# The ternary of the down weights in the first four neighbour steps of a fused GNN and FFN block, with later bias adds, earlier low parts and another ring of PSUM banks

## Chip, cores and metric

One Trainium2 chip, one of its cores. The metric is the device time of one execution in microseconds (us), the median of several runs. Lower is better. The engines are named as in the profile: PE is TensorE, DVE is VectorE, ACT is ScalarE, POOL is GpSimd and SP is SyncE, which here issues the DMAs.

## What is computed

```python
def _L0_gnn_ref(x, src, dst, W_self, W_neigh, b):          # x: 1250 x 512, 20000 edges
    msg_sum = jax.ops.segment_sum(x[src], dst, num_segments=N_NODES)
    deg = jax.ops.segment_sum(jnp.ones((src.shape[0],), x.dtype), dst, num_segments=N_NODES)
    neigh = msg_sum / jnp.maximum(deg, 1.0)[:, None]
    h = x @ W_self + neigh @ W_neigh + b
    h = jnp.where(h >= 0, h, LEAKY_SLOPE * h)
    norm = jnp.sqrt(jnp.sum(h * h, axis=1, keepdims=True))
    return h / jnp.maximum(norm, EPS)

def _quantize_weight(w, group_size):                       # groups of 128
    o, i = w.shape
    wg = w.reshape(o, i // group_size, group_size)
    scale = jnp.mean(jnp.abs(wg), axis=-1, keepdims=True) + EPS
    wq = jnp.clip(jnp.round(wg / scale), -1.0, 1.0) * scale
    return wq.reshape(o, i)

def _L0_ffn_ref(x, w_gate, w_up, w_down):                  # gate, up: 1408 x 512; down: 512 x 1408
    gate = _bitlinear(x, w_gate)
    up = _bitlinear(x, w_up)
    h = jax.nn.silu(gate) * up
    return _bitlinear(h, w_down)

x = x + _L0_gnn_ref(_layernorm(x, axis=-1), src, dst, L0_gnn_W_self, L0_gnn_W_neigh, L0_gnn_b)
x = x + _L0_ffn_ref(_layernorm(x, axis=-1)[None], L0_ffn_w_gate, L0_ffn_w_up, L0_ffn_w_down)[0]
```

## The kernel before

The 1250 nodes are ten tiles of 125 (NT = 10, TP = 125). The work has three stages. Each engine has its own program, written out by hand in the order of the code; semaphores tie them together, and every engine works strictly through its own list.

**Stage 1 (to about 121 us).** PE multiplies the normalized x by the two GNN weights (L1208) and builds a 1250 x 1250 matrix of edge counts, `a_t`, from one-hot matrices (L1167). `y` = x W_neigh is kept as a high and a low part (`y_hi`, `y_lo`), `z` = x W_self in SBUF. Beside it, the weights of the FFN are made ternary. They come in 34 loads of up to four blocks of 128 x 128 (jobs). For each job ACT takes the magnitudes and their sum (`abs_of`, L690), POOL makes from the sums of a load its thresholds (`scales_of`, L612), and DVE makes the ternary block (`ternary_of`, L901). Magnitudes have two slots (`MAGS`): those of a load wait for the ternaries of the load two before. Raw weights have four slots. Gate and up weights and the first 3 of 12 down loads are done in stage 1 (`LOADS1` = 25 loads); nine down loads (4, 3, 4, 4, 4, 3, 4, 4 and 3 jobs) are left. Their magnitudes go to `mag_late`, which may be written once the inverse degrees of the first six tiles are made (L1029, L1031).

**Stage 2, the neighbour steps (about 122 to 178 us).** For each node tile n, PE forms the neighbour sum of 20 matmuls (L1250) in bank 4 or 5. Then DVE, in step n: `neighbour_sum(n)` (L1040) adds the sum, divided by the degree, to `z`, for which POOL must have added the bias (L620); `residual(n - 1)` with `leak(n)` in its middle (L1046, L1058, bn_stats L1061, bn_aggr L1063); `shift1(n - 2)` (L1068, L1070); and the low part of a tile, `x1_low` (L1075). ACT, in step n: the square of tile n and its root (L785, L787), the root of the variance of tile n - 1 (L749), the high part of tile n - 3 (`x1_high`, L762), the normalizing of tile n - 2 (`normalize1`, L755). PE transposes normalized tile n - 3 after neighbour sum n (L1156).

The late ternaries are spread by `down_jobs(n)`: one load, then two, then one, and so on. ACT takes the magnitudes of `down_jobs(n)` at the end of step n, DVE the ternaries of `down_jobs(n - 1)` at the end of its step n. POOL adds all ten biases first and then makes the nine sets of thresholds:

```python
            for t in range(NT):
                pool.wait_ge(z_out, t + 1)
                nc.gpsimd.tensor_tensor(z[:, t, :], z[:, t, :], bias_b[0:TP, :], ALU.add).then_inc(z_done, 1)
            for l in range(LOADS1, len(loads)):
                scales_of(l)
```

**Stage 3, the FFN (from about 178 us).** The work is cut into 33 units (128 FFN columns by 3 or 4 node tiles) of 12 pieces (G0 to G3, U0 to U3, D0 to D3). Each piece is two matmuls (high and low part of the input, L1320) into one PSUM bank; ACT or DVE then takes it, scaled, into an accumulator (`take`, L808, L1114). Piece i uses bank `RING[i % 7]` and waits until piece i - 7 is taken. The first seven wait for what used the bank before, in a table in the code: banks 1 and 0 for the low parts of tiles 5 and 6 (`xlo_done` 6 and 7), banks 4 and 5 for neighbour sums 8 and 9 to be read (`hsum` 9 and 10), bank 3 for the last square, banks 2 and 6 for nothing that is late. Bank 7 carries the transposes of tiles 7 to 9 and of the ternary weights.

Of the kernel before, what the change touches and what calls it, by code (L numbers as in the profile page):

```python
# [31 lines left out]
ALU = mybir.AluOpType  # L32
# [11 lines left out]
def gnn_ffn(nc, x, src, dst, w_self, w_neigh, bias, w_gate, w_up, w_down, out):  # L44
# [3 lines left out]
    TP = 125  # L48
    NT = N // TP
# [55 lines left out]
    z = place("z", [TP, NT, D], F32, "xz")  # L105
# [62 lines left out]
    bias_b = small("bias_b", [P, D], F32)  # L168
# [21 lines left out]
    with ExitStack() as ctx:  # L190
# [72 lines left out]
        loads = []  # L263
# [70 lines left out]

        def down_jobs(n):

            lo, hi = (LOADS1 + max(0, min(NL, 3 * i // 2)) for i in (n, n + 1))
            return range(load_end[lo - 1], load_end[hi - 1])

# [39 lines left out]
        index = {p: i for i, p in enumerate(pieces)}  # L381
        RING = [2, 6, 1, 0, 4, 3, 5]
        added = {}
# [186 lines left out]
        def _(pool):  # L570
# [37 lines left out]
            def scales_of(l):  # L608

                js = slice(load_end[l] - loads[l][1], load_end[l])  # L610
                pool.wait_ge(abs_done, load_end[l])
                nc.gpsimd.tensor_scalar(thr[:, js], absum[:, js], 0.5 / P, 0.5 * Q_EPS, ALU.mult, ALU.add).then_inc(scales, 1)  # L612
# [4 lines left out]
            pool.wait_ge(joined, NB - 1)  # L617
            for t in range(NT):
                pool.wait_ge(z_out, t + 1)
                nc.gpsimd.tensor_tensor(z[:, t, :], z[:, t, :], bias_b[0:TP, :], ALU.add).then_inc(z_done, 1)  # L620
            for l in range(LOADS1, len(loads)):
                scales_of(l)

# [40 lines left out]
        def _(act):  # L664
# [111 lines left out]


            for n in range(NT):
                if n == NT - 1:
# [18 lines left out]
                if n == 0:  # L798
                    degree_out(2)
                for j in down_jobs(n):  # L800
                    abs_of(j)

# [66 lines left out]
        def _(dve):  # L869
# [203 lines left out]
            def x1_low(t):  # L1073
# [3 lines left out]
                                        ALU.subtract).then_inc(xlo_done, 1)  # L1077

            for n in range(NT):
                neighbour_sum(n)  # L1080
                if n >= 1:
                    residual(n - 1, between=n)
                else:
                    leak(n)
                if n >= 2:
                    shift1(n - 2)
                if n >= 4:
                    x1_low(n - 4)
                for j in down_jobs(n - 1):
                    ternary_of(j)  # L1090
                if n == 2:
                    inverse_degrees(DEG[2][0], DEG[2][1], 3, 2)
            shift1(NT - 2)
            x1_low(6)

# [250 lines left out]
```

## Time and profile before

| | |
|---|---|
| median of 3 runs | 363.95 us (363.95 to 364.2) |
| the profiled execution | 365.24 us |
| its span | 363.3 us |
| PE busy | 329.8 us (91%) |
| DVE busy | 304.6 us (84%) |
| ACT busy | 238.0 us (66%) |
| POOL busy | 163.1 us (45%) |

The chain that ended last is 58% PE, 26% DVE and 10% ACT; its largest lines are the FFN matmuls L1320 (39%) and L1208 (7%) and L1250 (5%). The profiled execution is 1.3 us longer than the median of the runs. A share of busy time is an average over three stages with different limits; the change lies in stage 2 and at the start of stage 3.

### The profile page before, as it was taken

Reading aid. Unit: us, or ns where it says so; the run is one execution under the profiler, and the core shown is the slowest. Engines: PE = TensorE matmul, PEld = TensorE weight load, DVE = VectorE, ACT = ScalarE, POOL = GpSimd, SP = SyncE. Lnnn points to the kernel's source line nnn. Section 1 sums busy time; section 2 is a strip of 40 time slices with the busy share of each in tenths; the row PEclk is TensorE's granted clock in tenths of the full one; section 3 lists DMA queues with packets and bytes.
Section 4 is the critical chain, followed back from the end, with each engine's and each line's share of the span. In section 5 each row is a group of like instructions: output and inputs, shape, how many; then the busy total and the mean of one; then the engine's idle time right before and its main releaser. Section 6 shows DMA issues by size and latency. Waiting matters only on the chain.

```text
span 363.3 us, 5834 instructions
## 1 busy us (share of the span) xinstructions
PE 329.8 (91%) x1623; PEld 249.6 (69%) x1623; DVE 304.6 (84%) x789; ACT 238.0 (66%) x637; POOL 163.1 (45%) x223
## 2 busy tenths in 40 slices
PE   1997879899999999999687999999999999999992
PEld 0443335554545578777476898989899898889991
DVE  3569999899889248999696998999999989999994
ACT  2155958899787136774656768668777678676670
POOL 7000000110010590110003466888788787799992
PEclk9999999999999999999988999999999999999998
DMA  7961322233232001200000000000000000000215
GB/s 226 291 159 33 86 58 78 68 88 87 59 82 79 3 3 35 74 22 2 0 1 2 0 3 0 3 0 0 2 3 2 0 0 3 0 3 0 73 44 169
DMA packets 9412, 16.69 MB, mean 46 GB/s; under 512 B 1062, under 2 KB 1886, under 8 KB 9378
## 3 DMA queue, kind: packets, MB, share of 16 engines
q1 hardware_dynamic: 9300, 16.21, 15.9%
q8 instruction: 14, 0.23, 0.3%
q14 instruction: 20, 0.16, 0.2%
q10 hardware_dynamic: 78, 0.08, 0.1%
HBM read 13.73 MB, written 2.56 MB: 45 GB/s over the span
## 4 chain that ended last, share of the span: by engine, by line
PE 58%; DVE 26%; ACT 10%; issue 3%; POOL 1%; DVEq 0%; ACTq 0%; POOLq 0%
PE bank L1320 39%; PE bank L1208 7%; PE bank L1250 5%; DVE tq_gu L901 4%; DVE hot_dst L1005 3%; ACT mag_early L690 3%; DVE tq_d L901 2%; DVE hot_src L996 2%; ACT a_t L742 2%; DVE bn L1061 2%; ACT hot_src L675 2%; DVE x_sb L1058 2%; DVE z L1040 1%; PE bank L1232 1%; PE bank L1156 1%
## 5 line engine op out<-in xcount | busy, mean ns | idle before, releaser
L1320 PE MATMUL bank<-x_hi,t_gu 128*128 128x378 f32 (+1 forms) x264 | 96.9, 367 | 3.6 <-DVE x_lo L1075 2.8
L1320 PE MATMUL bank<-x_lo,t_gu 128*128 128x378 f32 (+1 forms) x264 | 95.5, 362 | 0.0
L1208 PE MATMUL bank<-w_sb,xnT 128*125 128x512 f32 x160 | 86.9, 632 | 4.8 <-ACT z L725 4.1
L1114 DVE SCALAR_TENSOR_TENSOR g_acc<-bank,nscale,g_acc 128x378 f32<-128x378 f32 (+1 forms) x99 | 64.3, 650 | 12.1 <-PE bank L1320 10.8
L612 POOL TENSOR_SCALAR thr<-absum 128x4 f32<-128x4 f32 (+1 forms) x34 | 10.7, 315 | 121.5 <-ACT mag_early L690 97.2
L1114 DVE SCALAR_TENSOR_TENSOR u_acc<-bank,nscale,u_acc 128x378 f32<-128x378 f32 (+1 forms) x99 | 64.1, 647 | 0.0
L633 POOL TENSOR_TENSOR acc<-acc,d_one 128x378 f32<-128x378 f32 (+1 forms) x58 | 60.9, 1052 | 0.1
L643 POOL TENSOR_TENSOR hh<-sg,u_acc 128x378 f32<-128x378 f32 (+1 forms) x32 | 35.1, 1098 | 57.4 <-ACT sg L830 57.3
L1320 PEld LDWEIGHTS bank<-x_hi,t_gu 128*128 128x128 f32 x264 | 51.1, 193 | 8.1 <-DVE x_lo L1075 3.5
L1320 PEld LDWEIGHTS bank<-x_lo,t_gu 128*128 128x128 f32 x264 | 51.0, 193 | 3.6
L1167 PEld LDWEIGHTS bank<-hot_dst,hot_src 128*125 128x125 bf16 x157 | 20.8, 137 | 42.0 <-DVE hot_dst L1005 23.0
L1320 PE MATMUL bank<-h_hi,t_d 128*128 128x378 f32 (+1 forms) x132 | 48.2, 365 | 0.1
L1320 PE MATMUL bank<-h_lo,t_d 128*128 128x378 f32 (+1 forms) x132 | 46.6, 353 | 0.0
L1250 PE MATMUL bank<-y_hi,a_t 125*125 125x512 f32 x100 | 40.1, 401 | 0.8 <-DVE a_t L970 0.8
L690 ACT ACTIVATE mag_early<-raw 128x128 f32<-128x128 f32 x99 | 29.5, 301 | 16.8 <-DVE tq_gu L901 15.2
L1114 DVE SCALAR_TENSOR_TENSOR acc<-bank,nscale,acc 128x378 f32<-128x378 f32 (+1 forms) x62 | 39.5, 646 | 0.0
L1250 PE MATMUL bank<-y_lo,a_t 125*125 125x512 f32 x100 | 39.4, 394 | 0.0
L652 POOL TENSOR_TENSOR h_lo<-hh,h_hi 128x378 fp32r<-128x378 f32 (+1 forms) x32 | 35.1, 1096 | 3.4 <-ACT h_hi L847 1.9
L808 ACT ACTIVATE d_one<-bank,nscale 128x378 f32<-128x378 f32 (+1 forms) x58 | 35.2, 611 | 2.0 <-PE bank L1320 1.9
L808 ACT ACTIVATE g_acc<-bank,nscale 128x378 f32<-128x378 f32 (+1 forms) x33 | 20.2, 613 | 24.0 <-PE bank L1320 24.0
L1005 DVE TENSOR_SCALAR hot_dst<-iota_w,key 128x140 bf16<-128x140 uint16 (+4 forms) x150 | 34.2, 268 | 1.0 <-PE bank L1167 1.0
L1208 PEld LDWEIGHTS bank<-w_sb,xnT 128*125 128x125 f32 x160 | 25.4, 196 | 10.0 <-ACT z L725 5.1
(136 smaller groups left out, 558.5 us busy)
## 6 DMA issues: line engine op xcount, KB each, us to landing
raw<-in_L_ffn_w_gate SPq DMA_DIRECT2D x11, 256.0 KB, 2.7
raw<-in_L_ffn_w_up SPq DMA_DIRECT2D x11, 256.0 KB, 2.6
out_x<-x_sb SPq DMA_DIRECT2D x10, 224.0 KB
raw<-in_L_ffn_w_down SPq DMA_DIRECT2D x8, 256.0 KB, 2.7
x_sb<-in_x SPq DMA_DIRECT2D x1, 1344.0 KB
w_sb<-in_L_gnn_W_neigh SPq DMA_DIRECT2D x1, 1024.0 KB, 6.0
w_sb<-in_L_gnn_W_self SPq DMA_DIRECT2D x1, 1024.0 KB, 7.3
raw<-in_L_ffn_w_down SPq DMA_DIRECT2D x4, 192.0 KB, 2.3
```

The source lines that it names most:

```text
L633: nc.gpsimd.tensor_tensor(to, to, d_one[:, o, slot, 0:width(u)], ALU.add).then_inc(d_added, 1)
L643: nc.gpsimd.tensor_tensor(hh[:, u % 2, 0:w], sg[:, u % 2, 0:w], u_acc[:, u % 2, 0:w], ALU.mult).then_inc(h_done, 1)
L652: nc.gpsimd.tensor_tensor(h_lo[:, u % h_slots, 0:w], hh[:, u % 2, 0:w], h_hi[:, u % h_slots, 0:w].bitcast(F32), ALU.subtract).then_inc(hlo ...
L690: nc.scalar.activation(mag_of(j), raw_of(j), ACT.Abs, accum_out=absum[:, j:j + 1]).then_inc(abs_done, 1)
L808: nc.scalar.activation(to, bank_of(u, what)[:, 0:width(u)], ACT.Copy, scale=nscale[:, j:j + 1]).then_inc(act_took, 1)
L901: nc.vector.scalar_tensor_tensor(out=tq_of(j), in0=mag_of(j), scalar=thr[:, j:j + 1], in1=raw_of(j), op0=ALU.is_gt, op1=ALU.mult).then_inc ...
L1005: nc.vector.tensor_scalar(to, numbers, key[:, c:c + 1], None, ALU.is_equal).then_inc(hot_made, 1)
L1114: nc.vector.scalar_tensor_tensor(out=to, in0=bank_of(u, what)[:, 0:w], scalar=nscale[:, j:j + 1], in1=to, op0=ALU.mult, op1=ALU.add).then_ ...
L1167: nc.tensor.matmul(bank[k % 3][0:TP, 0:NT * WIN].rearrange("p (s d) -> p s d", d=WIN)[:, :, lo:hi], hot_src[:, c // SB % SBS, c % SB, 0:TP ...
L1208: last = nc.tensor.matmul(to[0:TP, :], xnT[:, t, k * TP:(k + 1) * TP], w_sb[:, k, half * D:(half + 1) * D], start=k == 0, stop=k == KD - 1)
L1250: last = nc.tensor.matmul(bank[4 + n % 2][0:TP, :], a_t[:, s, n * TP:(n + 1) * TP], y[:, s, :], start=s == 0 and y is y_hi, stop=s == NT - ...
L1320: last = nc.tensor.matmul(to, w, parts[h], start=h == 0, stop=h == 1)
```

## The change

The nine late loads are handed out by a list, `PHASE` = [3, 3, 2, 1]. Group 0 (three loads) stands on ACT and on DVE ahead of the neighbour steps; group n + 1 stands at the end of step n on both. POOL's bias adds stand one tile ahead of the steps, between the thresholds of the groups. The low part of tile n - 3 is made in DVE's step n, where it was that of tile n - 4. `RING` has another order.

```diff
-        def down_jobs(n):
-
-            lo, hi = (LOADS1 + max(0, min(NL, 3 * i // 2)) for i in (n, n + 1))
-            return range(load_end[lo - 1], load_end[hi - 1])
+        PHASE = [3, 3, 2, 1, 0, 0, 0, 0, 0, 0]
+        assert sum(PHASE) == NL
+
+        def late_loads(n):
+
+            lo = LOADS1 + sum(PHASE[:n])
+            return range(lo, lo + PHASE[n])
+
+        def late_jobs(n):
+
+            ls = late_loads(n)
+            return range(load_end[ls.start - 1], load_end[ls.stop - 1])
...
-        RING = [2, 6, 1, 0, 4, 3, 5]
+        RING = [2, 6, 4, 5, 3, 1, 0]
...
-            for t in range(NT):
-                pool.wait_ge(z_out, t + 1)
-                nc.gpsimd.tensor_tensor(z[:, t, :], z[:, t, :], bias_b[0:TP, :], ALU.add).then_inc(z_done, 1)
-            for l in range(LOADS1, len(loads)):
-                scales_of(l)
+            for n in range(-1, NT):
+                for t in range(0, 1) if n < 0 else range(n + 1, min(n + 2, NT)):
+                    pool.wait_ge(z_out, t + 1)
+                    nc.gpsimd.tensor_tensor(z[:, t, :], z[:, t, :], bias_b[0:TP, :], ALU.add).then_inc(z_done, 1)
+                if n >= 0:
+                    for l in late_loads(n):
+                        scales_of(l)
...
+            for j in late_jobs(0):
+                abs_of(j)
             for n in range(NT):
...
-                for j in down_jobs(n):
-                    abs_of(j)
+                if n < NT - 1:
+                    for j in late_jobs(n + 1):
+                        abs_of(j)
...
+            for j in late_jobs(0):
+                ternary_of(j)
             for n in range(NT):
                 neighbour_sum(n)
...
-                if n >= 4:
-                    x1_low(n - 4)
-                for j in down_jobs(n - 1):
-                    ternary_of(j)
+                if n >= 3:
+                    x1_low(n - 3)
+                if n < NT - 1:
+                    for j in late_jobs(n + 1):
+                        ternary_of(j)
                 if n == 2:
                     inverse_degrees(DEG[2][0], DEG[2][1], 3, 2)
             shift1(NT - 2)
-            x1_low(6)
```

What it does to the order of VectorE at the first neighbour steps, from the inverse degrees on (`z<-bank,rdeg,z` is the neighbour sum, `z<-z` the leak, `tq_d` the ternaries, `mv<-bn` bn_aggr). Before:

```order
502 L1031 RECIPROCAL rdeg<-rs 125x6 [waits rdeg_done]
503 L1040 SCALAR_TENSOR_TENSOR z<-bank,rdeg,z 125x512 [waits z_done,n_ready,rdeg_done]
504 L1046 SCALAR_TENSOR_TENSOR z<-z 125x512 [waits hsum]
505 L1040 SCALAR_TENSOR_TENSOR z<-bank,rdeg,z 125x512 [waits z_done,n_ready]
...
511 L1063 BN_AGGR mv_117<-bn 125x2 [waits bn_done]
512 L901 SCALAR_TENSOR_TENSOR tq_d<-mag_late,thr,raw 128x128 [waits scales] x4
513 L1040 SCALAR_TENSOR_TENSOR z<-bank,rdeg,z 125x512 [waits z_done,n_ready]
```

And in the changed kernel:

```order
502 L1043 RECIPROCAL rdeg<-rs 125x6 [waits rdeg_done]
503 L913 SCALAR_TENSOR_TENSOR tq_d<-mag_late,thr,raw 128x128 [waits scales,rdeg_done]
504 L913 SCALAR_TENSOR_TENSOR tq_d<-mag_late,thr,raw 128x128 [waits scales] x10
505 L1052 SCALAR_TENSOR_TENSOR z<-bank,rdeg,z 125x512 [waits z_done,n_ready]
506 L1058 SCALAR_TENSOR_TENSOR z<-z 125x512 [waits hsum]
507 L913 SCALAR_TENSOR_TENSOR tq_d<-mag_late,thr,raw 128x128 [waits scales] x11
508 L1052 SCALAR_TENSOR_TENSOR z<-bank,rdeg,z 125x512 [waits z_done,n_ready]
...
514 L1075 BN_AGGR mv_117<-bn 125x2 [waits bn_done]
515 L913 SCALAR_TENSOR_TENSOR tq_d<-mag_late,thr,raw 128x128 [waits scales] x8
516 L1052 SCALAR_TENSOR_TENSOR z<-bank,rdeg,z 125x512 [waits z_done,n_ready]
```

Eleven ternaries now stand ahead of neighbour sum 0, eleven ahead of sum 1 and eight ahead of sum 2, where there were none, none and four.

GpSimd after stage 1, where the bias adds are `z<-z,bias_b` and the thresholds `thr<-absum`. Before:

```order
57 L620 TENSOR_TENSOR z<-z,bias_b 125x512 [waits z_out,joined,bias_in]
58 L620 TENSOR_TENSOR z<-z,bias_b 125x512 [waits z_out] x9
59 L612 TENSOR_SCALAR thr<-absum 128x4 [waits abs_done]
60 L612 TENSOR_SCALAR thr<-absum 128x3 [waits abs_done]
61 L612 TENSOR_SCALAR thr<-absum 128x4 [waits abs_done] x3
```

And in the changed kernel:

```order
57 L628 TENSOR_TENSOR z<-z,bias_b 125x512 [waits z_out,joined,bias_in]
58 L628 TENSOR_TENSOR z<-z,bias_b 125x512 [waits z_out]
59 L619 TENSOR_SCALAR thr<-absum 128x4 [waits abs_done]
60 L619 TENSOR_SCALAR thr<-absum 128x3 [waits abs_done]
61 L619 TENSOR_SCALAR thr<-absum 128x4 [waits abs_done]
62 L628 TENSOR_TENSOR z<-z,bias_b 125x512 [waits z_out]
63 L619 TENSOR_SCALAR thr<-absum 128x4 [waits abs_done] x2
64 L619 TENSOR_SCALAR thr<-absum 128x3 [waits abs_done]
65 L628 TENSOR_TENSOR z<-z,bias_b 125x512 [waits z_out]
66 L619 TENSOR_SCALAR thr<-absum 128x4 [waits abs_done] x2
67 L628 TENSOR_TENSOR z<-z,bias_b 125x512 [waits z_out]
68 L619 TENSOR_SCALAR thr<-absum 128x3 [waits abs_done]
69 L628 TENSOR_TENSOR z<-z,bias_b 125x512 [waits z_out] x5
```

Two adds stand ahead of the thresholds, one behind each of the first three groups, and five behind the last threshold.

TensorE at the start of the FFN, the first matmul of each of the first pieces with its bank and its waits (the second matmuls are left out). Before:

```order
636 L1320 MATMUL bank2<-x1_hi_80,t_gu_88 128x378 [waits t_done,xlo_done,joined]
...
638 L1320 MATMUL bank6<-x1_hi_80,t_gu_88 128x378 [waits z_out]
...
640 L1320 MATMUL bank1<-x1_hi_80,t_gu_88 128x378 [waits xlo_done]
...
642 L1320 MATMUL bank0<-x1_hi_80,t_gu_88 128x378 [waits xlo_done]
...
644 L1320 MATMUL bank4<-x1_hi_80,t_gu_88 128x378 [waits hsum]
...
646 L1320 MATMUL bank3<-x1_hi_80,t_gu_88 128x378 [waits squares]
...
648 L1320 MATMUL bank5<-x1_hi_80,t_gu_88 128x378 [waits hsum]
```

And in the changed kernel:

```order
636 L1334 MATMUL bank2<-x1_hi_80,t_gu_88 128x378 [waits t_done,xlo_done,joined]
...
638 L1334 MATMUL bank6<-x1_hi_80,t_gu_88 128x378 [waits z_out]
...
640 L1334 MATMUL bank4<-x1_hi_80,t_gu_88 128x378 [waits hsum]
...
642 L1334 MATMUL bank5<-x1_hi_80,t_gu_88 128x378 [waits hsum]
...
644 L1334 MATMUL bank3<-x1_hi_80,t_gu_88 128x378 [waits squares]
...
646 L1334 MATMUL bank1<-x1_hi_80,t_gu_88 128x378 [waits xlo_done]
...
648 L1334 MATMUL bank0<-x1_hi_80,t_gu_88 128x378 [waits xlo_done]
```

The waits for low parts (`xlo_done`, banks 1 and 0) stand at the third and fourth piece before, and at the sixth and seventh now.

## Rows read from the trace of the kernel before

**Rows 1.** windows of the neighbour stage: length, then each engine's busy us (x instructions), granted clock

```profile
120.00:144.00 24.00, 23.24 (x105) 17.07 (x104) 11.97 (x31) 8.80 (x38) 13.85 (x13) 1.00 0.05 12
144.00:170.00 26.00, 25.26 (x120) 20.01 (x119) 25.24 (x77) 17.46 (x73) 2.81 (x7) 1.00 0.13 36
```

**Rows 2.** PE's waits from 120 to 206 us: engine, line, waited for: us, times, longest

```profile
PE bank L1156 <- ACT xn L755: 1.2, 2, 0.7
```

**Rows 3.** chain of work that ended last: start us, us, what

```profile
129.14 4.63 PE bank L1250 x20
```

**Rows 4.** PE's timeline, transposes of tiles 0 and 1: start us, us, instruction [idle <-releaser]

```profile
144.01 0.59 PE L1156 MATMUL bank<-ident,xn 126*128 126x126 f32 x4
149.97 0.65 PE L1156 MATMUL bank<-ident,xn 126*128 126x126 f32 x4 [0.74 <-ACT xn L755]
```

**Rows 5.** DVE's timeline, inverse degrees and neighbour steps 0 to 3

```profile
122.44 0.15 DVE L1029 TENSOR_SCALAR rs<-bank 125x6 f32<-125x6 f32 x1
126.98 0.75 DVE L1040 SCALAR_TENSOR_TENSOR z<-bank,rdeg,z 125x512 f32<-125x512 f32 x1 [4.16 <-PE bank L1250]
133.81 0.75 DVE L1040 SCALAR_TENSOR_TENSOR z<-bank,rdeg,z 125x512 f32<-125x512 f32 x1 [4.92 <-POOL z L620]
137.08 1.11 DVE L901 SCALAR_TENSOR_TENSOR tq_d<-mag_late,thr,raw 128x128 bf16<-128x128 f32 x4
139.59 0.75 DVE L1040 SCALAR_TENSOR_TENSOR z<-bank,rdeg,z 125x512 f32<-125x512 f32 x1 [1.41 <-PE bank L1250]
140.52 0.67 DVE L1046 SCALAR_TENSOR_TENSOR z<-z 125x512 f32<-125x512 f32 x1
142.61 0.18 DVE L1063 BATCH_NORM_AGGREGATE mv<-bn 125x2 f32<-125x6 f32 x1
145.20 0.75 DVE L1040 SCALAR_TENSOR_TENSOR z<-bank,rdeg,z 125x512 f32<-125x512 f32 x1
```

**Rows 6.** ACT's timeline, neighbour steps 0, 2 and 3

```profile
128.92 0.60 ACT L785 ACTIVATE bank<-z 125x512 f32<-125x512 f32 x1 [7.17 <-DVE z L1046]
130.25 0.29 ACT L690 ACTIVATE mag_late<-raw 128x128 f32<-128x128 f32 x1
131.33 0.19 ACT L690 ACTIVATION_READ_ACCUMULATOR mag_late<-raw 128x1 f32 x1
142.83 0.30 ACT L749 ACTIVATE sd<-mv,eps 125x1 f32<-125x1 f32 x1 [0.65 <-DVE mv L1063]
143.07 0.82 ACT L755 ACTIVATE xn<-x_sb,shift,rs 125x512 f32<-125x512 f32 x1
143.92 0.31 ACT L690 ACTIVATE mag_late<-raw 128x128 f32<-128x128 f32 x1
149.11 0.80 ACT L755 ACTIVATE xn<-x_sb,shift,rs 125x512 f32<-125x512 f32 x1
```

**Rows 7.** POOL's timeline, two of the bias adds

```profile
127.05 1.29 POOL L620 TENSOR_TENSOR z<-z,bias_b 125x512 f32<-125x512 f32 x1
128.30 1.74 POOL L620 TENSOR_TENSOR z<-z,bias_b 125x512 f32<-125x512 f32 x1
```

**Rows 8.** DVE's timeline, the leak of step 0

```profile
127.77 1.12 DVE L1046 SCALAR_TENSOR_TENSOR z<-z 125x512 f32<-125x512 f32 x1
```

**Rows 9.** window after a pause of PE, and PE's timeline in it

```profile
193.30:196.60 3.30, 3.30 (x15) 3.00 (x15) 1.91 (x3) 2.86 (x5) 0.17 (x1) 0.51 0.02 5
194.05 0.52 PE L1320 MATMUL bank<-x_lo,t_gu 128*128 128x378 f32 x1
194.37 0.52 PE L1320 MATMUL bank<-x_hi,t_gu 128*128 128x378 f32 x1
```

**Rows 10.** start of the FFN: PE's, ACT's and DVE's timelines

```profile
180.96 0.44 PE L1320 MATMUL bank<-x_hi,t_gu 128*128 128x378 f32 x1 [1.99 <-DVE x_lo L1075]
181.06 0.57 ACT L762 ACTIVATE x_hi<-bank 128x504 fp32r<-128x504 f32 x1
182.59 0.61 DVE L1114 SCALAR_TENSOR_TENSOR g_acc<-bank,nscale,g_acc 128x378 f32<-128x378 f32 x1 [0.24 <-ACT u_acc L808]
```

## The prediction, as it was made before the changed kernel ran

> **What bounds the kernel now.** I read the windows first. From 144 to 170 us VectorE is busy for 25.24 of 26.00 us and TensorE for 25.26; from 120 to 144 VectorE is busy for only 11.97 of 24 [rows 1]. So the sums start with a half empty VectorE and then fill it. The view of TensorE's waits shows how little that costs today: it waited twice for a normalized tile, 1.2 us in all, 0.7 the longer [rows 2]. The chain gives the pace of one neighbour sum: 20 matmuls in 4.63 us [rows 3]. TensorE's own rows show the two places that will matter: the transposes of normalized tile 0 start at 144.01, with no idle time ahead, and those of tile 1 at 149.97 after 0.74 us of waiting [rows 4]. TensorE is in order, so the fifth sum stands behind the first, the sixth behind the second. Tile 0 was normalized at 143.07 + 0.82 = 143.89 [rows 6], 0.1 us before TensorE wanted it. There is no slack on that path: whatever delays VectorE's third step (the one that begins with neighbour sum 2 at 139.59 [rows 5]) delays TensorE.
>
> **What the change does to the order.** Before, ScalarE took the magnitudes of a load in step n and VectorE the ternary of it in step n + 1, after its residual work: a lag of one step. Now both stand in the same step, and VectorE's ternaries stand ahead of the next neighbour sum. But ScalarE reaches those magnitudes only after the square of tile n and the root of tile n - 1, which need VectorE's leak and its bn_aggr of that very step. So VectorE now waits for ScalarE, which has just waited for VectorE, with GpSimd's scale in between. I call X0 to X3 the starts of VectorE's neighbour sums 0 to 3 (126.98, 133.81, 139.59 and 145.20 before [rows 5]) and work them out. Prices: four magnitudes take 130.25 to 131.52, 1.27 us, each further one 0.29 [rows 6]; four ternaries 1.11, three 0.85 [rows 5]; a scale with its hand-overs I put at 0.3; a bias add at 1.25 (from one start to the next) to 1.29 [rows 7].
>
> **The bias adds.** Ten adds ran in a row from 122.07 on, when VectorE had little to do. Where they met, both engines paid: the leak, whose two inputs lie in SBUF, took 1.12 us beside the add of 127.05, against 0.67 alone, and the next add took 1.74 against 1.29 [rows 5, 7, 8]. 127.77 + 0.45 is 128.2, just about where the first add ends, so the leak waited the add out. The Trainium skill, page "SBUF — State Buffer", section "Who interferes with whom", says that a VectorE instruction with two SBUF inputs and a GpSimd instruction that reads SBUF exclude each other for the whole instruction, the later one blocking fully. By that rule this change is charged for each add that it moves, the trace agrees (0.45 us on either side), and a mere sharing of bandwidth would give the smaller sum of the second rival. A ternary has two SBUF inputs as well. The new GpSimd order puts an add right behind the last scale of each group, so it starts as the ternaries of that load become ready: I charge VectorE one add (1.2 us) in each of the first three groups. From both sides: nothing if VectorE always goes first, 1.29 at most.
>
> **The sum.**
> - X0. Magnitudes of the first two late loads run 122.65 to 124.8, after the inverse degrees [rows 5]. Adds 0 and 1 end at 124.6, the scale at 124.85, ternaries run 124.9 to 126.8. The third load's magnitudes wait for a slot (there are two), which is free at 126.0: 126.05 to 127.35, scale 127.65, add 2 to 128.9, four ternaries to 130.0. **X0 = 130.0**; 128.8 without the collision. Harmless by itself: the third sum wants it at 134.7.
> - X1. The leak ends 1.46 later (126.98 to 128.89 is 1.91 [rows 5, 8], less the blocked 0.45), magnitudes start 1.36 after that (128.89 to 130.25 [rows 6, 8]): 132.8. The load's ternaries end at 135.5, which frees the slot for the group's third load: magnitudes to 136.5, scale 136.8, add 3 to 138.05, three ternaries. **X1 = 138.9** (136.5). The fourth sum wants it at about 139.4: still harmless.
> - X2. bn_aggr ends 3.20 after the start (139.59 to 142.79 [rows 5]), the root takes 0.25 [rows 6]; eight magnitudes 2.45, scale 0.3, add 4 1.2, four ternaries 1.1. **X2 = 147.4** (143.85).
> - Tile 0 is normalized at X2 + 4.30 [rows 5, 6] = 151.7, and TensorE goes on at 151.8 instead of 144.0: **+7.8** (+4.2).
> - X3. The ninth load's magnitudes start at X2 + 4.33 [rows 5, 6] = 151.75 and end at 152.7, scale 153.0. Now five adds in a row (6.3 us) meet three ternaries, the leak and the residual of x_sb. If an add slips in ahead of every ternary: 157.65, the inverse degrees 0.4 [rows 5], X3 = 158.05, the leak blocked for 1.2. Tile 1 is normalized 4.71 after X3 (145.20 to 149.91 [rows 5, 6]): 163.95. If the ternaries keep together, X3 = 155.5, and leak and residual lose 2.3: 162.5. I take the middle, **163.2** (155.4 without any collision), so TensorE's sixth sum is released at 163.3 instead of 149.97: **+13.3**. This contains the +7.8; the fifth sum ends before it and hides whatever it lost itself.
> - From X4 on TensorE needs 5.2 us for a step (149.97 less 144.01 and the wait of 0.74 [rows 4]) and VectorE some 4.6, although its low part now waits for the high part of the same step: that ends about when the normalizing starts, 3.9 after the sum on VectorE (145.20 to 149.11 [rows 5, 6]), and the low part takes some 0.7, like a leak. So TensorE sets the pace, and the waits of [rows 2] behind the first sums go: **-0.5** (1.2 less 0.7; the longer one is already in the comparison with 149.97).
> - The clock. Today's pauses of 2 us are followed by a stretch such as 193.3 to 196.6 at a granted 0.51, the 1.2 GHz level, with starts of 378 columns 0.32 apart; 0.232 for 512 columns makes 0.17 at the full level [rows 3, 9]. 3.3 us at the low level lose 1.4 to 1.5. The new pauses are three times as long, so I charge the sixth sum between one such stretch and two: **+2.0** (0 to 2.9).
> - The banks. TensorE gets its third to fifth pieces of the FFN without waiting 1.99 us for a low part [rows 10], but VectorE cannot add them: it must first make the low part of tile 6, whose high part starts on ScalarE at 181.06 as before, and its first piece is at 182.59 [rows 10]. One shift of tile 8 even moves behind that low part (0.15 us). From there to 192 VectorE and ScalarE set the pace, work which the change leaves in place. **0**, from -0.3 to +0.3. Every later piece still waits for the one seven before it.
>
> Together 13.3 - 0.5 + 2.0 + 0 = +14.8 us. The rows are of an execution of 365.24 us (span 363.3), 1.3 above the median of 363.95; the difference goes onto the median: **378.7 us**.
>
> **Rivals.**
> - *The adds cost little* (the engines share SBUF, or VectorE gets in first). The serial loop stays: the second transposes start at 155.5, +5.5, less 0.5, plus 0 to 1.4 for the clock: 369 to 370.4 us, say 369.5. For it: only one collision of this kind is in [rows 7, 8]. Against: both engines lost 0.45 there, as in a full wait. Chance 0.13.
> - *The gaps swallow it* (the other side: faster). The early ternaries lie in the idle half of [rows 1]; if VectorE began neighbour sum 2 by 139.7, tile 0 would be on time, later steps would be free of ternaries, the 1.2 us of [rows 2] would vanish and perhaps 0.3 with the banks: 362.5 us. It decides at 139.7. Against: even from an undelayed X1 of 133.81 the loop of bn_aggr, root, eight magnitudes, scale and four ternaries takes 7.3 us and ends at 141.1. Chance 0.04.
> - *The pauses grow*: both low stretches count in full, every add blocks 1.29, and the start of the FFN runs at the low level too: 380.5 to 383 us. Chance 0.10.
>
> **How the numbers follow.** The forecast has 0.73, with 376 to 381 as its own range. The range for 8 in 10 takes in the first rival, since its cause is the least certain price: 369 to 381.5. A measurement here can tell about 0.2%, 0.7 us. Faster 0.04, same 0.01, slower 0.95.
>
> **What would show it.** In the changed trace: VectorE idle before ternaries in the first three steps, waiting for GpSimd's scales; its neighbour sums 0 to 3 starting near 130, 139, 147 and 156 to 158; TensorE idle for over 6 us ahead of the first transposes of a normalized tile and again ahead of the second; granted clock at half behind them; bias adds and ternaries stretched where they meet; from the sixth sum on a pace of 5.2 us. From the first unit of the FFN to the end the duration stays within 0.5 us. Wrong if neighbour sum 2 starts on VectorE before 141, if TensorE waits under 3 us in this stage, or if the FFN part changes by over a microsecond.

## The result, and the profile after

| | before | changed |
|---|---|---|
| median of 4 runs each | 364.07 us | 378.4 us (378.26 to 379.22) |
| ratio, 95% interval | | 1.0379 (1.0358 to 1.0401) |
| span of the profiled execution | 363.3 us | 376.4 us |

The kernel became slower by 14.3 us; 378.7 us had been predicted. The page of the changed kernel:

```profile
span 376.4 us, 5835 instructions
...
PE 332.6 (88%) x1623; PEld 251.4 (67%) x1623; DVE 311.6 (83%) x789; ACT 238.1 (63%) x637; POOL 161.7 (43%) x223
```

The engines are as busy as before to within 7 us (DVE 311.6 against 304.6, and those 7 us are time in which VectorE's instructions were blocked, as will be seen). What the kernel lost is mostly waiting. TensorE's waits from 118 to 215 us (engine, line, waited for: us in all, times, longest) answer to [rows 2]:

```profile
PE bank L1170 <- ACT xn L764: 11.6, 2, 7.0
PE bank L1246 <- DVE x_lo L1087: 3.2, 1, 3.2
PE bank L1334 <- DVE x_lo L1087: 2.0, 1, 2.0
```

Twice TensorE waits for a normalized tile, as before, but for 11.6 us and not 1.2. TensorE's timeline shows both, and answers to [rows 4]:

```profile
150.53 1.10 PE L1170 MATMUL bank<-ident,xn 126*128 126x126 f32 x4 [7.03 <-ACT xn L764]
...
161.87 1.10 PE L1170 MATMUL bank<-ident,xn 126*128 126x126 f32 x4 [4.59 <-ACT xn L764]
```

To compare the stages, I count from the first neighbour matmul on TensorE to neighbour sum 9 on VectorE, and from there to the end. Stage 1, which has the same program in every kernel of this study, ended at anything from 120.7 to 123.6 us in the profiled executions; it explains nothing of the change, but it does move the time of a single execution by a microsecond or two. In the trace of before (PE's and DVE's timelines):

```profile
121.98 0.50 PE L1250 MATMUL bank<-y_hi,a_t 125*125 125x512 f32 x1 [0.76 <-DVE a_t L970]
```

```profile
176.86 0.75 DVE L1040 SCALAR_TENSOR_TENSOR z<-bank,rdeg,z 125x512 f32<-125x512 f32 x1 [2.15 <-PE bank L1250]
```

and in that of the changed kernel:

```profile
120.89 0.49 PE L1264 MATMUL bank<-y_hi,a_t 125*125 125x512 f32 x1 [0.76 <-DVE a_t L982]
```

```profile
190.57 0.75 DVE L1052 SCALAR_TENSOR_TENSOR z<-bank,rdeg,z 125x512 f32<-125x512 f32 x1 [0.86 <-PE bank L1264]
```

The neighbour stage took 54.88 us and takes 69.68, **14.80 us more**; the rest took 363.3 - 176.86 = 186.44 and takes 185.83, **0.61 us less**. The sum is 14.19, the medians differ by 14.33.

The inside of the stage is in VectorE's timeline, which answers to [rows 5] (L913 are the ternaries, L1052 the neighbour sums, L1058 the leak):

```profile
123.90 1.93 DVE L913 SCALAR_TENSOR_TENSOR tq_d<-mag_late,thr,raw 128x128 bf16<-128x128 f32 x7 [2.17 <-POOL thr L619]
126.73 2.27 DVE L913 SCALAR_TENSOR_TENSOR tq_d<-mag_late,thr,raw 128x128 bf16<-128x128 f32 x4 [0.90 <-POOL thr L619]
128.92 0.73 DVE L1052 SCALAR_TENSOR_TENSOR z<-bank,rdeg,z 125x512 f32<-125x512 f32 x1
...
133.33 2.37 DVE L913 SCALAR_TENSOR_TENSOR tq_d<-mag_late,thr,raw 128x128 bf16<-128x128 f32 x8 [2.94 <-POOL thr L619]
135.87 2.01 DVE L913 SCALAR_TENSOR_TENSOR tq_d<-mag_late,thr,raw 128x128 bf16<-128x128 f32 x3 [0.17 <-POOL thr L619]
137.80 0.74 DVE L1052 SCALAR_TENSOR_TENSOR z<-bank,rdeg,z 125x512 f32<-125x512 f32 x1
...
142.81 3.47 DVE L913 SCALAR_TENSOR_TENSOR tq_d<-mag_late,thr,raw 128x128 bf16<-128x128 f32 x8 [1.82 <-POOL thr L619]
146.20 0.74 DVE L1052 SCALAR_TENSOR_TENSOR z<-bank,rdeg,z 125x512 f32<-125x512 f32 x1
...
151.67 4.07 DVE L913 SCALAR_TENSOR_TENSOR tq_d<-mag_late,thr,raw 128x128 bf16<-128x128 f32 x3 [2.04 <-POOL thr L619]
...
156.06 0.75 DVE L1052 SCALAR_TENSOR_TENSOR z<-bank,rdeg,z 125x512 f32<-125x512 f32 x1
...
156.99 1.68 DVE L1058 SCALAR_TENSOR_TENSOR z<-z 125x512 f32<-125x512 f32 x1
```

VectorE now idles before every group of ternaries until GpSimd's scale comes (2.17, 2.94, 1.82 and 2.04 us in front of the first of each group); GpSimd itself waits there for ScalarE's magnitudes. And some groups take much longer than their work. The neighbour sums 0 to 3 start 8.03, 16.91, 25.31 and 35.17 us after the first neighbour matmul; before it was 5.00, 11.83, 17.61 and 23.22.

GpSimd in the same stretch, which answers to [rows 7]; the last row is the five adds in a row:

```profile
126.77 1.29 POOL L628 TENSOR_TENSOR z<-z,bias_b 125x512 f32<-125x512 f32 x1
...
135.91 1.29 POOL L628 TENSOR_TENSOR z<-z,bias_b 125x512 f32<-125x512 f32 x1
...
144.08 1.26 POOL L628 TENSOR_TENSOR z<-z,bias_b 125x512 f32<-125x512 f32 x1
...
151.72 6.40 POOL L628 TENSOR_TENSOR z<-z,bias_b 125x512 f32<-125x512 f32 x5
```

The last group at close range: VectorE's first ternary, then the other two, and the first of the adds.

```profile
151.67 1.47 DVE L913 SCALAR_TENSOR_TENSOR tq_d<-mag_late,thr,raw 128x128 bf16<-128x128 f32 x1 [2.04 <-POOL thr L619]
```

```profile
153.07 2.67 DVE L913 SCALAR_TENSOR_TENSOR tq_d<-mag_late,thr,raw 128x128 bf16<-128x128 f32 x2
```

```profile
151.72 1.28 POOL L628 TENSOR_TENSOR z<-z,bias_b 125x512 f32<-125x512 f32 x1
```

An add starts 0.05 us after the first ternary; that ternary then lasts 1.47 us instead of 0.35 and ends 0.15 us after the add, which took its usual 1.28. The second and third together end at 155.74, each of them 0.15 us after the next add. One ternary passes for each add.

And the clock after the second pause, in a window that answers to [rows 9] (length; busy us of PE, PEld, DVE, ACT and POOL; granted clock; DMA share; GB/s):

```profile
162.50:167.20 4.70, 4.70 (x14) 3.71 (x13) 3.22 (x9) 2.40 (x6) 0.00 (x0) 0.50 0.00 0
```

For 4.7 us the sixth sum ran at the lower of the two levels (0.50 granted, 1.2 GHz).

### The profile page after: what moved, and what is told of

It reads as the page before. It is cut to its first block, busy times and chain, and to the rows that moved or that the text cites. A ratio compares the mean times of both kernels' runs of the same rounds, so it can differ in the third digit from the quotient of the medians.

```text
span 376.4 us, 5835 instructions
## 1 busy us (share of the span) xinstructions
PE 332.6 (88%) x1623; PEld 251.4 (67%) x1623; DVE 311.6 (83%) x789; ACT 238.1 (63%) x637; POOL 161.7 (43%) x223
## 4 chain that ended last, share of the span: by engine, by line
PE 55%; DVE 21%; ACT 12%; issue 7%; POOL 3%; DVEq 0%; ACTq 0%; POOLq 0%
PE bank L1334 38%; PE bank L1264 7%; PE bank L1222 4%; DVE tq_gu L913 3%; ACT mag_early L699 3%; DVE hot_dst L1017 3%; DVE tq_d L913 2%; ACT mag_late L699 2%; PE bank L1170 2%; ACT a_t L751 2%; DVE hot_src L1008 2%; ACT hot_src L684 1%; PE bank L1246 1%; DVE bn L899 1%; DVE z L1058 1%
## 5 line engine op out<-in xcount | busy, mean ns | idle before, releaser
L1334 PE MATMUL bank<-x_hi,t_gu 128*128 128x378 f32 (+1 forms) x264 | 95.8, 363 | 2.8 <-DVE x_lo L1087 2.0
L1334 PE MATMUL bank<-x_lo,t_gu 128*128 128x378 f32 (+1 forms) x264 | 94.5, 358 | 0.0
L619 POOL TENSOR_SCALAR thr<-absum 128x4 f32<-128x4 f32 (+1 forms) x34 | 9.2, 270 | 118.3 <-ACT mag_early L699 96.1
L1334 PEld LDWEIGHTS bank<-x_hi,t_gu 128*128 128x128 f32 x264 | 50.3, 191 | 7.0 <-DVE x_lo L1087 2.3
L1264 PE MATMUL bank<-y_hi,a_t 125*125 125x512 f32 x100 | 42.4, 424 | 0.8 <-DVE a_t L982 0.8
L1264 PE MATMUL bank<-y_lo,a_t 125*125 125x512 f32 x100 | 41.2, 412 | 0.0
L699 ACT ACTIVATE mag_early<-raw 128x128 f32<-128x128 f32 x99 | 29.5, 301 | 17.6 <-DVE tq_gu L913 14.8
L1170 PE MATMUL bank<-ident,xn 125*128 125x125 f32 (+1 forms) x80 | 13.5, 295 | 21.5 <-ACT xn L764 11.6
```

Source lines behind the costliest of these rows:

```text
L699: nc.scalar.activation(mag_of(j), raw_of(j), ACT.Abs, accum_out=absum[:, j:j + 1]).then_inc(abs_done, 1)
L1170: last = nc.tensor.transpose(to[:, k * n:(k + 1) * n], xn[0:n, t % 2, k * P:(k + 1) * P], ident[0:n, 0:n])
L1264: last = nc.tensor.matmul(bank[4 + n % 2][0:TP, :], a_t[:, s, n * TP:(n + 1) * TP], y[:, s, :], start=s == 0 and y is y_hi, stop=s == NT - ...
L1334: last = nc.tensor.matmul(to, w, parts[h], start=h == 0, stop=h == 1)
```

## The experiments

All times are medians; the kernel before was run beside each group, at 364.1 to 365.0 us, so the ratio is the better guide. The two last columns are of one profiled execution each. "Stage" is the neighbour stage as counted above (54.88 before, 69.68 changed).

| kernel | median, us | ratio to before (95%) | stage, us | stage end to end of span |
|---|---|---|---|---|
| changed | 378.4 | 1.0379 (1.0358 to 1.0401) | 69.68 | 185.83 |
| short adds | 369.26 | 1.0127 (1.0102 to 1.0152) | 59.74 | 185.91 |
| magnitudes first | 368.9 | 1.0116 (1.0057 to 1.0175) | 58.83 | 185.72 |
| both | 362.96 | 0.9956 (0.994 to 0.9971) | 53.53 | 185.85 |
| old ring, old low parts | 378.79 | 1.0368 (1.032 to 1.0416) | 68.53 | 186.45 |
| adds wait for ternaries | 372.0 | 1.019 (1.0164 to 1.0216) | 61.95 | 186.19 |
| before + ring | 364.85 | 1.0003 (0.9988 to 1.0018) | 54.87 | 185.96 |
| before + low parts | 368.38 | 1.0098 (1.0077 to 1.0119) | 58.22 | 186.54 |
| before + bias adds | 370.61 | 1.0158 (1.0131 to 1.0185) | 61.13 | 186.52 |
| two early loads | 366.48 | 1.0052 (1.0034 to 1.0069) | 57.77 | 185.85 |
| two early loads, adds wait | 362.7 | 0.9938 (0.9919 to 0.9957) | 53.61 | 186.02 |

### The changed kernel with short adds

```diff
-                    nc.gpsimd.tensor_tensor(z[:, t, :], z[:, t, :], bias_b[0:TP, :], ALU.add).then_inc(z_done, 1)
+                    m = D if t < 2 else 8
+                    nc.gpsimd.tensor_tensor(z[:, t, 0:m], z[:, t, 0:m], bias_b[0:TP, 0:m], ALU.add).then_inc(z_done, 1)
```

> The changed kernel, but GpSimd's bias adds of tiles 2 to 9 cover only 8 of the 512 columns, in the same places of its program: this leaves out the bias of the other columns of these tiles. My theory (two causes: the serial loop of ScalarE, GpSimd and VectorE in each step, and the collisions of adds with VectorE instructions that have two SBUF inputs): the ternary groups lose their stretched first instruction, neighbour sum 2 starts on VectorE some 3.6 us sooner, the second transposes 7.5 to 8 us sooner, and TensorE is slow for a shorter time: 369.5 to 370.5 us. Rival (the loop alone is the cause, the adds only happen to lie beside it): 376 to 378 us, and the time from the scale to the end of the ternaries does not change.

Measured 369.26 us, 0.2 below the forecast range. Neighbour sum 2 started on VectorE 3.25 us sooner (22.06 us into the stage and not 25.31) and the second transposes 7.4 us sooner. VectorE's groups of 4, 3 and 3 ternaries that an add had met (2.27, 2.01 and 4.07 us in the changed kernel):

```profile
127.78 1.18 DVE L914 SCALAR_TENSOR_TENSOR tq_d<-mag_late,thr,raw 128x128 bf16<-128x128 f32 x4 [0.90 <-POOL thr L619]
...
135.83 0.92 DVE L914 SCALAR_TENSOR_TENSOR tq_d<-mag_late,thr,raw 128x128 bf16<-128x128 f32 x3 [0.17 <-POOL thr L619]
...
149.48 0.92 DVE L914 SCALAR_TENSOR_TENSOR tq_d<-mag_late,thr,raw 128x128 bf16<-128x128 f32 x3 [2.04 <-POOL thr L619]
```

The collisions cost 9.9 us of the stage (69.68 less 59.74), TensorE's slower clock behind longer pauses included. The rival falls. The edit takes work off GpSimd as well as the collisions; the kernel with full adds that wait, below, tells the two apart.

### The changed kernel with the magnitudes first

```diff
+                if n < NT - 1:
+                    for j in late_jobs(n + 1):
+                        abs_of(j)
                 act.wait_ge(leaky, n + 1)
...
-                if n < NT - 1:
-                    for j in late_jobs(n + 1):
-                        abs_of(j)
```

> The changed kernel, but ScalarE takes the magnitudes of group n + 1 at the start of its step n, ahead of the square, in place of the end, so they no longer wait for VectorE's leak and bn_aggr. Full adds. My theory: the loop is cut, the collisions stay. VectorE's neighbour sum 2 starts some 6 us sooner, the two long pauses of TensorE shrink to under 2 us each; about 1 us is lost because the degree row goes out later on ScalarE: 367 to 369.5 us. Rival (the mere amount of ternary work ahead of the sums, or the collisions alone, cause the loss): 375 us or more.

Measured 368.9 us (367.36 to 371.32). TensorE's waits:

```profile
PE bank L1170 <- ACT xn L764: 2.3, 2, 2.0
...
PE bank L510 <- ACT deg_row L704: 1.2, 1, 1.2
```

The two pauses are 2.3 us in all instead of 11.6, and the degree row costs the 1.2 us that were foreseen. Neighbour sum 2 starts on VectorE 142.97 - 123.55 = 19.42 us into the stage and not 25.31. So cutting the loop alone gives back 10.9 us of the stage, with the collisions in place. The amount of ternary work and its place ahead of the sums are unchanged in this kernel, so they are not the cause of those 10.9 us; whether they cost any of the other 3.9 the next kernel tells. The four runs of this one lie further apart than those of any other here, from 0.8% to 1.9% above before.

### Both edits

> Both edits of the two runs before in one kernel (the bias of tiles 2 to 9 beyond column 8 is left out). If loop and collisions are all of the loss, nothing is left: VectorE's neighbour sum 2 starts when TensorE has it ready, no long pause remains, and the later steps are light: 362 to 363.5 us, below the kernel before. If something else also costs (a third cause, such as the slots of the magnitudes or the low parts), it stays above 365 us.

Measured 362.96 us, 0.44% below before (0.29% to 0.60%). TensorE's waits for normalized tiles in the neighbour stage are gone; what is left of its waits is at the start of the FFN:

```profile
PE bank L1171 <- ACT t_gu L782: 2.1, 1, 2.1
PE bank L1335 <- DVE x_lo L1088: 2.0, 1, 2.0
PE bank L1247 <- DVE x_lo L1088: 1.9, 1, 1.9
```

The stage is 53.53 us. Loop and collisions are all of the loss, and without them the spread of the ternaries gains 1.35 us of stage. Alone, the edits give back 9.9 and 10.9 us, together 16.2 and not 20.8: they overlap. A pause of TensorE that one of them shortens can't be shortened again, and each of them alone already brings the clock back (tile 1's transposes to neighbour sum 5 on VectorE take 7.85 us in the changed kernel, 5.3 in each of the three).

### The changed kernel with full adds that wait

```diff
+                    if 1 <= n <= 4:
+                        pool.wait_ge(ternary, load_end[late_loads(n - 1).stop - 1])
                     pool.wait_ge(z_out, t + 1)
```

> The changed kernel with its full bias adds, but each add or row of adds behind a group's scales waits until the ternaries of the group are done. Nothing is left out. The loop stays; the collisions with ternaries go, those with leaks and the residual stay (about 0.5, 0.35 and 0.35 us in steps 0 to 2, some 2 in step 3, where five adds run in a row): 372 to 374.5 us, between the changed kernel and the one with shortened adds. If the collisions with ternaries were harmless: 378 us.

Measured 372.0 us, at the lower edge of the range. With full adds and the whole computation in place, the ternaries take their bare time:

```profile
127.80 1.14 DVE L915 SCALAR_TENSOR_TENSOR tq_d<-mag_late,thr,raw 128x128 bf16<-128x128 f32 x4 [0.90 <-POOL thr L619]
...
129.64 1.23 DVE L1060 SCALAR_TENSOR_TENSOR z<-z 125x512 f32<-125x512 f32 x1
...
136.35 0.88 DVE L915 SCALAR_TENSOR_TENSOR tq_d<-mag_late,thr,raw 128x128 bf16<-128x128 f32 x3 [0.16 <-POOL thr L619]
...
150.73 0.88 DVE L915 SCALAR_TENSOR_TENSOR tq_d<-mag_late,thr,raw 128x128 bf16<-128x128 f32 x3 [2.04 <-POOL thr L619]
```

The second row is the leak of step 0, which now meets the add in place of the ternary (1.23 us against 0.67). That shows that it is the meeting that costs, not the work of the add as such: of the 9.9 us that short adds gave back, a wait gives back 7.7 (stage 61.95) with all the work in place. The other 2.2 us lie with adds that now meet leaks and a residual; that share was not taken apart.

### The changed kernel with the old ring and the old low parts

> The changed kernel with the old ring of banks and the low part of tile n - 4 in step n, so that only the ternary groups and the bias adds differ from before. My theory: these two parts carry all of the loss. The ring gave back about 0.5 us at the start of the FFN, the earlier low parts cost nothing where TensorE sets the pace: 378.4 to 379.4 us. Rival (the earlier low parts, which make VectorE wait for the high part of the same step, cost part of it): below 377.5 us.

Measured 378.79 us (376.1 to 379.1), as expected: the ternary groups and the bias adds carry the loss. The stage of the profiled execution is 1.15 us shorter, but not through the low parts: tile 1's transposes start 40.98 us into the stage in both kernels. TensorE's sixth sum is at the low level for a shorter time: its last stretched matmul starts at 165.40, 2.6 us after the transposes that end the pause, and in the changed kernel at 167.03, 5.2 us after those of 161.87. TensorE's timelines, of this kernel:

```profile
162.80 1.10 PE L1171 MATMUL bank<-ident,xn 126*128 126x126 f32 x4 [4.16 <-ACT xn L764]
...
165.40 0.60 PE L1265 MATMUL bank<-y_hi,a_t 125*125 125x512 f32 x1
```

and of the changed one:

```profile
167.03 0.56 PE L1264 MATMUL bank<-y_hi,a_t 125*125 125x512 f32 x1
```

### The kernel before with one part each

Ring alone (`RING = [2, 6, 4, 5, 3, 1, 0]`):

> The kernel before with the new ring of banks alone. From the trace of the changed kernel, where the time from neighbour sum 9 on VectorE to the end is 0.6 us shorter: 363.4 to 363.6 us, about 0.5 us gained, because TensorE's pieces of the first unit are ready when VectorE gets to them, at the full clock. Rival, as the prediction had it: VectorE and ScalarE set the pace there, nothing is gained, 363.7 to 364.3 us.

Measured 364.85 us in 12 runs that lay between 363.08 and 366.46, ratio 1.0003 (0.9988 to 1.0018), above both forecast ranges, as before itself was beside it (364.62). The half microsecond that was forecast does not show in the time; it does in the traces. From neighbour sum 9 to the end, the four profiled kernels with the old ring took 186.44 to 186.54 us, the eight with the new one 185.72 to 186.19. The least difference is 0.25, that of the means 0.6 us; between this kernel and before, which differ in the ring alone, it is 0.48.

Low parts alone (`x1_low(n - 3)` from step 3 on):

> The kernel before with the low part of tile n - 3 in step n alone. In the old order VectorE's steps of 4 and 7 ternaries are as long as TensorE's, so the wait for the high part of the same step (some 0.6 us in steps 3 to 7) has nothing to hide in: 366 to 367.5 us. Rival: TensorE has enough in hand, 363.7 to 364.5 us.

Measured 368.38 us, 0.9 above the range; the stage is 3.34 us longer, in a profiled execution that was 1.1 above the median. TensorE now waits for low parts in the stage itself (the row of four waits), as the transposes of tile t wait for the low part of tile t - 2, whose bank they use:

```profile
PE bank L1155 <- DVE x_lo L1075: 3.3, 4, 1.2
```

In the changed kernel the same edit cost nothing that shows (378.4 us with it, 378.79 without). Its steps from 4 on have no ternaries, which is the likely reason.

Bias adds alone, one tile ahead of the steps (scales of 1, 2, 1, 2, 1, 2 loads between them):

> The kernel before with the bias adds one tile ahead of the steps alone, between the scales of the old groups (1, 2, 1, 2, 1, 2 loads). My theory: each add behind a scale meets a leak, a residual or a ternary on a VectorE that has no slack in steps 2 to 8, each 0.3 to 1 us: 365 to 367.5 us. Rival (the collisions need the five adds in a row, or a ternary that waits for the scale ahead of them): within 0.5 us of before.

Measured 370.61 us, **3 us above the range**. The direction and mechanism were right, the size was not. VectorE's timeline, two leaks or residuals (L1049, L1061) and the last group of seven ternaries:

```profile
146.06 1.28 DVE L1049 SCALAR_TENSOR_TENSOR z<-z 125x512 f32<-125x512 f32 x1
...
158.03 1.79 DVE L1061 SCALAR_TENSOR_TENSOR x_sb<-z,inv,x_sb 125x512 f32<-125x512 f32 x1
...
166.77 3.58 DVE L904 SCALAR_TENSOR_TENSOR tq_d<-mag_late,thr,raw 128x128 bf16<-128x128 f32 x7
```

I had charged single collisions. The last three adds come in a row, and two of them meet the seven ternaries of step 6: 3.58 us instead of 1.92. VectorE is then late for TensorE's transposes; TensorE waits for normalized tiles four times, 5.4 us in all:

```profile
PE bank L1159 <- ACT xn L758: 5.4, 4, 2.3
```

### Two loads early, one in each later step

```diff
-            lo, hi = (LOADS1 + max(0, min(NL, 3 * i // 2)) for i in (n, n + 1))
+            lo, hi = (LOADS1 + max(0, min(NL, EARLY + i)) for i in (n, n + 1))
+            if n < 0:
+                lo, hi = LOADS1, LOADS1 + EARLY
...
             for t in range(NT):
+                if t == 2:
+                    for l in range(LOADS1, LOADS1 + EARLY):
+                        scales_of(l)
                 pool.wait_ge(z_out, t + 1)
```

with `EARLY = 2`, `down_jobs(-1)` ahead of the steps on ScalarE and VectorE, and the new ring.

> A new order: the kernel before with the new ring, two loads made ternary ahead of neighbour sum 0, in VectorE's first gap, and one load in each later step with the old lag of one step; GpSimd makes the two scales behind its second bias add, the other adds as before, in a row. The first group costs one collision (VectorE's neighbour sum 0 near 128, where TensorE wants the bank at 134.7), no step has seven ternaries, so the waits of 0.7 and 0.4 us for normalized tiles go: 362 to 363 us. Rival: the time is set elsewhere, 363.4 us as with the ring alone.

Measured 366.48 us against 364.62 of before beside it: **a miss**, slower and not faster. VectorE's and GpSimd's timelines and TensorE's wait:

```profile
123.78 8.19 DVE L909 SCALAR_TENSOR_TENSOR tq_d<-mag_late,thr,raw 128x128 bf16<-128x128 f32 x7 [2.16 <-POOL thr L615]
```

```profile
124.03 10.75 POOL L626 TENSOR_TENSOR z<-z,bias_b 125x512 f32<-125x512 f32 x8
```

```profile
PE bank L506 <- ACT deg_row L701: 2.5, 1, 2.5
```

Seven ternaries, 1.9 us of work, took 8.19 us. I had charged one collision for the group. But GpSimd has eight adds in a row there. The first ternary came just ahead of them, and each of the other six waited for an add of its own. Neighbour sum 0 started at 131.89, the degree row after it was late, and TensorE waited 2.5 us for it. From neighbour sum 2 to sum 9 this kernel takes 178.55 - 142.67 = 35.88 us, where before takes 37.27: the light later steps did bring their 1.4 us.

So GpSimd's third add was made to wait for the seven ternaries:

```diff
+                if t == 2:
+                    pool.wait_ge(ternary, load_end[LOADS1 + EARLY - 1])
                 pool.wait_ge(z_out, t + 1)
```

> The order with two loads made ternary ahead of neighbour sum 0, but GpSimd's third to tenth bias add wait until those seven ternaries are done. In the run without that wait each ternary alternated with an add (8.2 us for seven), neighbour sum 0 started on VectorE near 132 and TensorE waited 2.5 us for the degree row. My theory, alternation: the seven ternaries now take 1.9 us, neighbour sum 0 starts when TensorE has it, no wait of TensorE is left in the stage, which takes 53.5 us from the first neighbour matmul to neighbour sum 9 on VectorE, where before has 54.9: 361.9 to 362.9 us, 0.3 to 0.6% below the kernel before of the same runs. Rival (the two early loads themselves are in the way): 364 us or more.

Measured 362.7 us against 364.98 of before beside it, 0.62% faster (0.43% to 0.81%); each of its six runs was below each of the eleven of before. This version beats both kernels with the whole computation in place. Rows of its VectorE timeline (the early group, the leak of step 0 and the residual of tile 0) and of TensorE's waits from 118 to 215 us:

```profile
124.48 1.93 DVE L911 SCALAR_TENSOR_TENSOR tq_d<-mag_late,thr,raw 128x128 bf16<-128x128 f32 x7 [2.17 <-POOL thr L615]
...
127.20 1.13 DVE L1056 SCALAR_TENSOR_TENSOR z<-z 125x512 f32<-125x512 f32 x1
...
134.92 1.78 DVE L1068 SCALAR_TENSOR_TENSOR x_sb<-z,inv,x_sb 125x512 f32<-125x512 f32 x1
```

```profile
PE bank L1245 <- DVE x_lo L1085: 2.8, 1, 2.8
PE bank L1333 <- DVE x_lo L1085: 1.7, 2, 0.9
```

The seven ternaries take 1.93 us and the leak meets an add as it always did. As the adds end later now, a residual meets one too (1.78 us against 0.74), but no wait of TensorE follows from it: those that are left are of the FFN's start.

## Why the prediction was right, point by point

**X0 to X3.** Predicted 130.0, 138.9, 147.4 and about 157, on the clock of the trace of before; the stage began 1.09 us earlier in the changed trace, so 128.92, 137.80, 146.20 and 156.06 stand for 130.01, 138.89, 147.29 and 157.15. The order of events was the one described: VectorE waits in each step for scales, and the third load of a group for a slot. Two of the signs that the prediction named for this stage did not come: TensorE's second pause was to be over 6 us like the first and was 4.59, and adds were to be stretched where they meet ternaries, but took 1.26 to 1.34 us.

**The loop and the adds as two causes.** Shown by the two edits, alone and together, and by full adds that wait. In the first three groups an add cost VectorE 1.16, 1.13 and 1.06 us (2.27 less the 1.11 of before, 2.01 less the 0.88 of the kernel whose adds wait, and 3.47 less 2.41 in the kernel with short adds), for the 1.2 charged. For the row of five adds the prediction took the middle between one blocked ternary and three. It was three (4.07 us), and the leak was blocked too (1.68), as in the upper bound, but each step of that chain was a little shorter than charged: X3 is 157.15 and not 158.05. That the sum met the middle is luck.

**The releases.** Tile 0's transposes 7.8 us late: 150.53 + 1.09 - 144.01 = 7.61. Tile 1's 13.3 us late: 161.87 + 1.09 - 149.97 = 12.99. Both are 0.2 to 0.3 less than charged.

**The clock**, +2.0: from tile 1's transposes to neighbour sum 5 on VectorE TensorE's work took 7.85 us (161.87 to 169.72) and before 5.43 (149.97 to 155.40), so the term is +2.42. Eleven matmuls of the sixth sum start at the low level (162.62 to 167.03), 0.43 us apart instead of 0.23, and the transposes before them are slower too. The size is luck in part, since the kernel with the old ring shows 1.1 us less behind a like pause.

**The stage**: predicted 13.3 - 0.5 + 2.0 = +14.8. Measured are 12.99 for the release, 2.42 for the clock and -0.61 for the four steps from neighbour sum 5 to 9 (20.85 us against 21.46): 14.80 in all. The terms were each right to 0.1 to 0.4 us, and their errors cancel: an agreement of the sum to 0.01 is luck.

**The banks**, 0 (-0.3 to +0.3): this step was mis-sized. It gains 0.6 us in this trace and 0.48 with the ring alone, and the prediction's sign that the FFN would stay within 0.5 us just failed. VectorE's first piece did come no sooner (5.70 us after its neighbour sum 9, 5.73 before), as argued. What the argument missed lies behind it, and TensorE's clock may be the link. Before, the two waits for low parts (1.99 us ending at 180.96, and the next piece's 0.84) were followed by a low stretch (granted 0.68 from 184 to 188) in which the first unit's pieces came later than VectorE could take them. With one wait in place of two TensorE went on at the full level (granted 1.00 from 194.7 to 197.7): the residual step of tile 9 starts 8.83 us after neighbour sum 9 and not 9.06. The low stretch was not spared, it came later, behind a wait of 3.2 us (granted 0.60 from 201.7 to 205.7). By the transposes of tile 9 the difference is 0.53 (21.13 against 21.66 us). The ring is shown to be the cause of the gain; that the low stretch is behind the first 0.23 of it is only read from the timelines, since no run changed the clock alone, and the rest was not traced.

**The rivals.** Adds without cost, the first of the list (the text on the bias adds calls it the second rival): 369.5, which is what the kernel with short adds took (369.26); so the price of that case was right, and the case did not hold. The prediction granted it that the trace of before had a single collision. It had a second, the leak of step 1 beside the last add (133.74 to 135.01):

```profile
134.74 0.82 DVE L1046 SCALAR_TENSOR_TENSOR z<-z 125x512 f32<-125x512 f32 x1
```

It ends at 135.56 (134.74 + 0.82), 0.55 us after its add, and so does the leak of step 0, which ends at 128.89, after the add that ended at 128.34. The same lag in both, for waits of different length, is what waiting out an add looks like. The gaps swallow it: the kernel with both edits shows what it would have taken, 362.96, close to the 362.5 worked out.

**The SBUF page.** The Trainium skill, page "SBUF — State Buffer", section "Who interferes with whom", has the later instruction wait for the whole of the earlier one. The runs agree that one excludes the other (VectorE lost 0.1 to 1.1 us each time, up to the end of the add). The neighbour sums, which read one of their two tensors from a PSUM bank, took 0.75 us beside adds, as alone. Which of the two is the earlier can't be told from recorded starts that lie close together: the first blocked ternary of each of the four groups has its recorded start 0.04 to 0.05 us before that of its add, and it is the ternary that waits. The runs add what happens to a queue on either side, which is the next section but one.

## What to carry to other kernels

Before work is moved into an engine's idle gap, follow its inputs: if they come from an engine that waits for the first one in the same step, the gap is a round trip and not free time. Here a lag of one step was worth more than an earlier place. On VectorE and GpSimd, count for each long GpSimd instruction on SBUF one VectorE instruction with two SBUF inputs that waits for it; a group of short ternaries beside a row of adds pays once for each ternary. A wait on GpSimd's side can be the cure: it brought 366.48 us to 362.7, where the delayed adds then met nothing that TensorE waited for, and 378.4 to 372.0 in the changed kernel, where they met leaks and a residual and the loop stayed.

## What the hardware showed that was not expected

The two engines alternate when both have a queue. Seven short ternaries beside eight adds took 8.19 us where seven of them alone take 1.93, and three took 4.07 beside five adds: some 1.3 us for each blocked ternary, the length of one add. So short instructions suffer most for their length. That splitting VectorE's work into smaller pieces would make it worse follows from this, but no run tried it. Beside ternaries the adds lose little: five take 6.40 us, against 5 x 1.25 = 6.25 undisturbed. Beside a leak an add loses more (1.74 us against 1.29 [rows 7]).

The low clock after a pause does not last equally long in two executions. After pauses of 4.59 and 4.16 us of TensorE, in the changed kernel and in that with the old ring, the last slow matmul started 5.2 and 2.6 us after work resumed, and the second pause cost 2.4 and 1.3 us by it. Such a cost should be given as a range.
